# Raw q weights in other buffers, and the output weights loaded during the first step

## The reference

```python
x = x + tanh(g_xattn[0]) * xattn(layernorm(x), ctx)
x = x + tanh(g_ffn[0]) * ffn(layernorm(x))

# xattn
ln_out = ln(hidden) * ln_w + ln_b
q, k, v, qx = [einsum(fp8(clip(ln_out / s)) * s, w) * w_scale  for the four weights]
q, k, qx = ln(...) per head of 128            # 16 q heads, 8 k and v heads
core = softmax(q k / sqrt(128)) v
kx, vx = split(cond @ w_kv_x);  kx = ln(kx)
xout = softmax(qx kx / sqrt(128)) vx
catq = fp8(clip(concat(core, xout) / proj_smooth))
return catq @ wproj * (proj_in_scale * proj_w_scale)

# ffn: 16 experts, the best 2 per token, and a shared expert
out = sum_e combine[:, e] * (silu(x @ Wu[e]) * (x @ Wg[e])) @ Wd[e]  +  shared
```

## Time and profile before

| | us |
|---|---|
| median of 3 runs | 509.16 (497.39, 510.69, 509.16) |
| the profiled execution | 494.47 |
| its span, first to last instruction | 492.6 |
| PE busy | 416.0 (84%) |
| DVE busy | 372.3 (76%) |
| ACT busy | 281.5 (57%) |
| POOL busy | 277.5 (56%) |
| chain that ended last, PE's share | 41% |
| the same, DVE's and POOL's shares | 19% and 13% |
| the same, DMA of the output weights | 3% |

### The profile page before, as it was taken

How to read it: one execution, slowest core, us unless ns; L and a number is a source line. 1 busy time by engine, 2 the same in 40 slices (tenths; PEclk the granted TensorE clock), 3 DMA queues, 4 the chain that set the end, 5 groups by cost and what they waited for, 6 DMA issues and landing times.

```text
span 492.6 us, 9942 instructions
## 1 busy us (share of the span) xinstructions
PE 416.0 (84%) x2982; PEld 311.5 (63%) x2982; DVE 372.3 (76%) x832; ACT 281.5 (57%) x610; POOL 277.5 (56%) x401
## 2 busy tenths in 40 slices
PE   0588823999999999999999999999988499999930
PEld 0446513776777677677677677777677387787820
DVE  5988760899999999989999989999978662232335
ACT  3679921666767776776677677676870322232320
POOL 2064480468677686766865965864550471266660
PEclk9999975999999999999999999999998699999975
DMA  8930069999970000000000000000093132343308
GB/s 211 276 133 1 1 80 212 275 278 275 243 192 0 0 0 0 0 0 0 0 0 0 0 0 0 0 1 1 10 414 155 45 106 86 81 131 116 107 20 256
DMA packets 34810, 45.66 MB, mean 93 GB/s; under 512 B 3034, under 2 KB 32223, under 8 KB 33888
## 3 DMA queue, kind: packets, MB, share of 16 engines
q1 hardware_dynamic: 26656, 35.61, 24.6%
q0 software_dynamic: 6992, 9.46, 8.8%
q10 hardware_dynamic: 1136, 0.27, 0.3%
HBM read 28.34 MB, written 24.32 MB: 107 GB/s over the span
## 4 chain that ended last, share of the span: by engine, by line
PE 41%; DVE 19%; POOL 13%; issue 11%; ACT 7%; DMA 6%; ACTq 1%; POOLq 1%; SPq 0%; DVEq 0%
PE proj_ps L860 9%; PE score_ps L887 7%; PE proj_ps L1017 6%; PE pv_ps L909 4%; DMA wp_sb<-in_wpT 3%; PE out_ps L919 3%; POOL xin L501 3%; POOL rot L529 3%; POOL zbuf L570 3%; DVE st L1243 3%; DVE yv L1270 2%; ACT rot L647 2%; PE headT_ps L878 2%; PE probT_ps L895 2%; ACT qT L682 2%
## 5 line engine op out<-in xcount | busy, mean ns | idle before, releaser
L860 PE MATMUL proj_ps<-arena 128*128 128x512 f16 x384 | 100.3, 384 | 19.8 <-DMA wp_sb<-in_wpT 16.4
L1243 DVE BATCH_NORM_STATS2 st<-rot 128x6 f32<-128x256 f32 x192 | 72.7, 420 | 28.4 <-ACT rot L647 27.4
L647 ACT ACTIVATE rot<-proj_ps 128x512 f32<-128x512 f32 x96 | 56.5, 588 | 36.9 <-PE proj_ps L860 35.3
L535 POOL TENSOR_TENSOR reg<-reg,rinv 128x512 f32<-128x512 f32 x32 | 34.6, 1080 | 65.8 <-DVE rinv L1263 65.8
L529 POOL TENSOR_TENSOR rot<-rot,cw 128x512 f32<-128x512 f32 x64 | 67.4, 1074 | 2.5
L860 PEld LDWEIGHTS proj_ps<-arena 128*128 (+1 forms) x384 | 37.5, 103 | 45.7 <-issue 22.5
L887 PE MATMUL score_ps<-kT,qT 128*128 128x64 f32 x512 | 62.1, 275 | 0.6 <-ACT qT L682 0.5
L887 PEld LDWEIGHTS score_ps<-kT,qT 128*128 128x128 f32 x512 | 60.3, 194 | 2.4 <-ACT qT L682 2.3
L668 ACT ACTIVATE rot<-rot,cw 128x128 f32<-128x128 f32 x128 | 40.9, 390 | 29.0 <-POOL cw L523 29.0
L852 PE MATMUL proj_ps<-arena 128*128 128x512 f16 x192 | 46.7, 379 | 0.0
L589 POOL DMA_INDIRECT ybuf<-arena,bslot x32 | 31.5, 984 | 24.7 <-DVE arena L1447 19.1
(11 more groups left out here) (221 smaller groups left out, 860.0 us busy)
## 6 DMA issues: line engine op xcount, KB each, us to landing
zbuf<-fill SPq DMA_DIRECT2D x1, 16576.5 KB, 65.9
arena<-in_wffn SPq DMA_DIRECT2D x4, 1536.0 KB, 13.6
arena<-zbuf SPq DMA_DIRECT2D x32, 128.5 KB, 2.1
wkv_stage<-in_wkvN SPq DMA_DIRECT2D x1, 2048.0 KB, 14.8
wp_sb<-in_wpT POOLq DMA_DIRECT2D x1, 2048.0 KB, 15.6
wp_sb<-ybuf SPq DMA_DIRECT2D x8, 256.0 KB, 4.4
xs<-in_x SPq DMA_DIRECT2D x2, 512.0 KB, 5.5
wp_sb<-in_wqN POOLq DMA_DIRECT2D x1, 1024.0 KB, 12.8
```

The costliest lines, as they stand in the source:

```text
L647: act.activation(raw[c % 2][i], proj_ps[i % 2][:, :], ACT.Copy).then_inc(proj_evac, 1)
L860: mm = pe.matmul(ps, lhs, w[kind][:, ch, 512 * b:512 * b + 512], start=(k == 0), stop=(k == 3))
L1243: ins = ve.bn_stats(st[:, 4 * i + h:4 * i + h + 2, :].rearrange("p h s -> p (h s)"), raw[c % 2][i][:, h * D:(h + 2) * D].rearrange("p (h d ...
```

## The change

The raw q weights lie in `vv` in place of the first half of `wp`, and the raw qx weights in columns 4096 to 8191 of `arena`, where the rounded inputs of tiles 4 to 7 come later. Nothing then lies in `wp`, and the load of the output weights is issued at the end of GpSimd's step n = 0 in place of n = 2. It waits for the landing of the cross weights in place of the end of the folds. Shapes, bytes and arithmetic are as before.

```diff
-        wpf = wp[:, :, :].rearrange("p h o -> p (h o)")
-        wraw = {"q": wpf[:, 0:4096], "qx": wpf[:, 4096:8192],
+        wraw = {"q": vv[:, :, :].rearrange("p a t -> p (a t)").bitcast(BF16),
+                "qx": arena[:, 4096:8192].bitcast(BF16),
                 "k": kT[:, :, :, :].rearrange("p a h t -> p (a h t)").bitcast(BF16),
                 "v": qT[:, 0, :, :].rearrange("p h t -> p (h t)").bitcast(BF16)}
...
             def load_output_weights():
 
-                gp.wait_ge(fold_done, ON_PE[4 * NFOLD])
+                gp.wait_ge(ld_wkv, 16)
                 gp.dma_start(wp[:, :, :], wpT.rearrange("(h p) o -> p h o", p=P)).then_inc(ld_wp, 16)
...
-                if isinstance(n, int) and n == 2:
+                if isinstance(n, int) and n == 0:
                     load_output_weights()
```

## The result

The changed kernel takes 479.25 us (median of 4 runs, 476.56 to 480.3) against 503.27 us before (4 runs, 494.35 to 510.69). Two of those four runs of before, 509.16 and 510.69 us, were in a slower state of the chip and are left out of the ratio, which is therefore not the quotient of the two medians. The ratio is 0.9657, with a 95% interval of 0.957 to 0.9743. Of the 495.9 us that the other two take in the mean, that is 17.0 us, with an interval of 12.7 to 21.3. Two later comparisons gave 0.9689 (0.9603 to 0.9776) and 0.9644 (0.9591 to 0.9698).

What follows compares the result with a forecast made beforehand. TensorE was taken as full except while waiting 16.4 us for the output weights. Stall 15.87 plus low clock 1.43 gave 17.3, taken as 17.2; 509.16 less 17.2 is 491.9 us, range 476 to 499, chance 0.86.

Steps and rivals of the forecast that it cites:

- The stall: TensorE's wait for the output weights before tile 1: start at 65.44 in place of 81.31, 15.87 us gained.
- The low clock: Tile 1 behind the stall: 1.43 us longer than a settled tile, taken as the price of the low granted clock.
- The bound from below, 15.9: Low bound of the gain, 15.9 us, if tile 1 stays as long as it is.
- Sum: Whole gain between the input roundings of tiles 0 and 1: 17.2 us, all other parts counted as 0.
- The high bound: Gain of 18.2 us, because the interval holds one step without an output product, whose eight matmuls take 1.05 us.
- Issue at no cost: GpSimd's 1.77 us issue in step 0 fits 1.84 us without work and leaves VectorE's folds unstretched: cost 0.
- Rival B: GpSimd's issue held in the first step until VectorE runs dry: 9.8 us more, 501.7 us; chance 0.05.
- The new wait and the landing: GpSimd's wait for the cross weights costs 0; the load lands at 55.5 to 63.4, before 65.44.
- The fill: The big table's fill on the SP queue starts some 11 us earlier, near 70, beside tile 1: cost 0.
- Rival C: Clock falls in settled tiles, making it slower: two whole tiles at low clock cost 29 us, 521 us; chance 0.04.
- Rival D: Load issued or landing late, TensorE still stands at line 1006: 500 us for half the stall, 509 full; chance 0.05.
- The level: Whole-kernel starting time, the median of the runs shown, 509.16 us, from which 17.2 was taken to give 491.9.

Runs made afterwards that it cites:

- The buffers alone: The changed kernel with the output-weight load put back behind the last fold, raw weights in their new buffers: ratio to before 0.9965, median 499.83 against 503.12 us.
- The warm stall: The kernel before with 72 matmuls of 512 columns put into TensorE's stall, results overwritten: ratio 0.9908, median 498.07 against 503.12 us.
- the comparison of five rounds: The changed kernel unaltered against the kernel before, run beside one with 8 and 10 extra matmuls: ratio 0.9644, median 479.67 us.

## Why the prediction was right, point by point

- *The stall.* Right in place and size: TensorE starts tile 1 at 65.14, where 65.44 was said, 0.28 of the difference being the start. The buffers alone leave the stall whole, and the issue in step 2 moves it by what the landing moves. That shows the landing as the cause.
- *The low clock.* Right as a mechanism, the size was a net of two: 1.78 us for the clock less 0.34 us that the other engines gain by getting ahead, together the 1.43 counted. That the net came out is luck in part, since only the sum of the two could be read from before. The warm stall parts them. And it is no constant: with the same stall, one execution paid 42.69 - 38.77 = 3.92 us. The bound from below, 15.9, took this price as nothing, and no execution showed that.
- *Sum.* 17.2 said, 17.32 between the two roundings. The ratio gives 17.0 us, but its interval of 12.7 to 21.3 couldn't have told the sum from either bound; it is the rows that do. The high bound (the missing output product, 1.05 us) was not used: GpSimd's rounding, and not TensorE's work, lets tile 1 begin, and TensorE waits 0.52 us for it.
- *Issue at no cost.* Right, with 0.15 us to spare on GpSimd, and VectorE's folds at 1.39 us. Rival B did not come, and the rows narrow it: the issue took 1.77 us in eleven of the twelve executions, also beside the 16-bit operation at 65.6, and 1.75 in the one that issues at the start. It was VectorE that got longer. The prediction compared 1.62 us with the 0.43 "elsewhere"; at that place in a tile the operation takes 1.15 us without any issue too, beside GpSimd's `normalise`. In both cases it ends 0.2 to 0.3 us behind GpSimd's instruction (67.23 behind 67.01, 66.46 behind 66.18). The rule of the Trainium skill, page "SBUF — State Buffer", section "Who interferes with whom", that the second to come is blocked, agrees with this, since here VectorE was the second. Whether an issue that comes second is held is not shown: in the kernel before it begins at 65.24, within a 16-bit operation of VectorE (line 1203, 64.94 to 65.58), and takes its 1.77 us, but GpSimd's own rounding ran beside that operation until 65.30 and may have held it up.
- *The new wait and the landing.* Right, and the cover was wider than it had to be: with the issue at 3.6 tile 0's rounding comes at 61.71, within the scatter of the start (60.2 to 61.9), and nothing behind it is later.
- *The fill.* Started at 68.67 where about 70 was said. Under it tile 1 took 39.11 us.
- *Rival C* (clock in settled tiles): it was 1.00 in them. Rival D: no wait for the weights.
- *The level.* 491.9 was said and 479.25 measured. It lies inside the range, but 12.7 us below the value, and the failed term is the level of before: the median of three runs, 509.16, was near the high end of a kernel whose later medians were 503.27, 503.12, 498.0 and 499.61; the two runs that the ratio leaves out made it so. The 17.2 subtracted from it were right. From the profiled execution, 494.47 - 17.2 = 477.3 would have been nearer.

**What stays open.** The times of one kernel vary by several us, before and after: over all runs shown from 493.78 to 513.66 for the kernel before and from 476.36 to 489.31 for the changed one, but these are 41 runs against 14, and in the comparison of five rounds the two spread alike (8.3 and 8.0 us). Two parts were seen, the price of the low clock behind the stall (1.8 and 3.9 us) and the clock in the router stage; no execution of above 501 us was profiled. Also open is whether the issue at the end of step 1 costs anything: its one profiled execution had the clock low in the router stage (0.63 and 0.50 in the 10 us from 340 on) and the longer way to the first block, which can't be told from chance.

## What to carry to other kernels

A load that TensorE waits for in full is worth its stall plus the low clock behind it, here 16 and some 2 us, and it is enough that it lands before the next wait in line: landings half a microsecond, 10 and 25 us ahead gave the same start of tile 1, within the scatter of the start. Look for buffers that are dead at the start before making a big load wait for its own buffer. For the absolute time take the level from the execution whose rows are summed, or from more than three runs.

## What the runs showed of the hardware that I had not expected

- A load of 2 MB into SBUF, issued by GpSimd at 3.6 us, left the loads of its own queue ahead of it and those of the SP queue beside it as they were: context 13.8 us to landing with and without it, cross weights 15.4 against 15.1, raw qx 23.6 both times; the load itself took 36.9 instead of 15.6.
- The low clock after an idle stretch of 16.4 us lasted to different lengths in two executions: granted 0.63 and then 1.00 in the two stretches of 5 us behind it, or 0.50 and 0.68. Behind 5.6 us of idle time it was 0.61 in the first stretch.
- A VectorE operation of 16 bits within SBUF, 0.43 us long elsewhere, that started while GpSimd issued the load or ran `normalise` ended 0.2 to 0.3 us behind GpSimd's instruction: it took 1.62 us beside the issue and 1.15 beside `normalise`.
- Short rests in the router stage, 2.0 us at 340, were followed by a low clock in one execution (0.66) and not in another (1.00).
